# Sums of |d| by output products of two heads at a time, with |d| from ScalarE, and the rotary sum on VectorE

## The reference

```python
attn_exp = softmax(s1); attn_noise = softmax(s2)      # s1 = q k1 * SCALE, s2 = q k2 * SCALE, causal
attn = attn_exp - lam * attn_noise
denom = jnp.maximum(jnp.sum(jnp.abs(attn), axis=-1, keepdims=True), 1e-06)
attn = attn / denom
out = jnp.einsum('bhqk,bhkd->bhqd', attn, v)
```

```python
q = q * cos * scale + rotate_half(q) * sin * scale
k = k * cos / scale + rotate_half(k) * sin / scale
```

## Time and profile before

| | |
|---|---|
| median of three runs | 2244.88 us |
| profiled execution | 2240.0 us, span 2238.2 us |
| TensorE matmul busy | 1963.2 us, 88% |
| VectorE busy | 1743.6 us, 78% |
| ScalarE busy | 1389.7 us, 62% |
| GpSimd busy | 618.9 us, 28% |
| differential attention | about 36 to 794 us |
| window attention, first layer | about 816 to 1187 us |
| window attention, second layer | about 1284 to 1657 us |

### The profile page before, as it was taken

How to read it: one execution, slowest core, us unless ns; L and a number is a source line. 1 busy time by engine, 2 the same in 40 slices (tenths; PEclk the granted TensorE clock), 3 DMA queues, 4 the chain that set the end, 5 groups by cost and what they waited for, 6 DMA issues and landing times. The chain is left out here.

```text
span 2238.2 us, 43106 instructions
## 1 busy us (share of the span) xinstructions
PE 1963.2 (88%) x12640; PEld 1328.9 (59%) x12706; DVE 1743.6 (78%) x4650; ACT 1389.7 (62%) x4626; POOL 618.9 (28%) x494
## 2 busy tenths in 40 slices
PE   5999999999999947999996869999969384999998
PEld 3666656665666625777774537777745242666665
DVE  3989989899998967999993659999956737666666
ACT  2878778787787845888882338888843526333232
POOL 1101001010010135555561255555532403000000
PEclk9999999999998968999998969999989786999999
DMA  6000000000000000000001000000001000000000
GB/s 189 1 2 1 1 1 1 1 1 1 1 1 1 1 4 6 14 14 9 14 14 28 20 5 15 11 13 14 14 19 29 5 0 1 6 5 5 5 9 10
DMA packets 40718, 27.41 MB, mean 12 GB/s; under 512 B 23954, under 2 KB 33810, under 8 KB 40594
## 3 DMA queue, kind: packets, MB, share of 16 engines
q1 hardware_dynamic: 40594, 26.24, 4.5%
HBM read 10.51 MB, written 2.10 MB: 6 GB/s over the span
## 5 line engine op out<-in xcount | busy, mean ns | idle before, releaser
L391 ACT ACTIVATE a_E<-a_psS,a_nm 128x128 f32<-128x128 f32 (+1 forms) x1028 | 418.9, 429 | 29.1 <-DVE a_nm L210 29.1
L210 DVE TENSOR_REDUCE a_nm<-a_psS 128x2 f32<-128x256 f32 (+1 forms) x514 | 260.3, 548 | 58.0 <-PE a_psS L475 56.7
L471 PE MATMUL a_psS<-a_kT,a_qm 32*128 32x128 f32 (+1 forms) x2064 | 249.0, 360 | 1.9 <-ACT a_E L391 0.8
L391 ACT ACTIVATION_READ_ACCUMULATOR a_E<-a_psS,a_nm 128x1 f32 x1028 | 221.4, 215 | 0.0
L180 POOL TENSOR_TENSOR a_rs<-a_mv,minus_half 128x2 f32<-128x2 f32 x34 | 23.9, 703 | 683.6 <-DVE a_mv L260 683.6
L399 ACT ACTIVATE a_dT<-a_psT 128x384 f32<-128x384 f32 x256 | 125.8, 491 | 135.4 <-PE a_psT L484 134.1
L235 DVE SCALAR_TENSOR_TENSOR a_d<-a_E,a_cf 128x128 f32<-128x128 f32 (+1 forms) x512 | 196.4, 425 | 8.5
L1553 ACT ACTIVATE mx_sl<-mx_psG 128x512 f32<-128x512 f32 x128 | 76.1, 597 | 197.9 <-PE mx_psG L1731 197.1
L471 PEld LDWEIGHTS a_psS<-a_kT,a_qm 32*128 32x128 f32 x2064 | 140.4, 192 | 48.7 <-ACT a_E L391 28.1
L484 PE MATMUL a_psT<-ident,a_d 128*128 128x128 f32 x768 | 136.9, 289 | 32.0 <-DVE a_d L235 30.8
L792 POOL TENSOR_TENSOR b0rn<-b0ss,minus_half 128x16 f32<-128x16 f32 x36 | 107.6, 2989 | 128.3 <-DVE b0ss L832 128.3
(11 more groups left out here) (303 smaller groups left out, 4943.8 us busy)
## 6 DMA issues: line engine op xcount, KB each, us to landing
b0v<-b0v SPq DMA_DIRECT2D x34, 128.0 KB, 2.3
b1v<-b1v SPq DMA_DIRECT2D x34, 128.0 KB, 2.3
out_dram<-mx_res SPq DMA_DIRECT2D x8, 256.0 KB, 2.3
f0z<-F SPq DMA_DIRECT2D x9, 128.0 KB
f1z<-F SPq DMA_DIRECT2D x9, 128.0 KB
f0z<-F SPq DMA_DIRECT2D x9, 127.0 KB
f1z<-F SPq DMA_DIRECT2D x9, 127.0 KB
wqk<-in_wqkv_dram SPq DMA_DIRECT2D x2, 512.0 KB, 4.6
```

The lines of the kernel that those rows point to most:

```text
L210: ins = dve.tensor_reduce(nm[:, s, t, :], psS[:, s, :, (0, P)[t]:(P, 384)[t]], axis=AX.X, op=ALU.max, negate=True)
L391: ins = act.activation(E[:, s, m, c0:c1], psS[:, s, m, c0:c1], ACT.Exp, bias=nm[:, s, t, m:m + 1], accum_out=Z[:, p, h, t, m:m + 1])
L471: pe.matmul(psS[:, s, m, c0:c1], qm[rows, p, a, r, t * P:(t + 1) * P], kT[rows, p, a, 0:c1 - c0], start=(t == 0), stop=False)
```

## The change

In differential attention, |d| is no longer summed by VectorE. ScalarE evacuates psT twice, once with Copy to dT and once with Abs to a new tile aT. TensorE multiplies aT by a stationary tile `ones`, which is 1 in column 8 and 0 elsewhere, into the same psO partitions as the outputs, so that column 8 of a head's 32 is the sum of |d|. The outputs of heads h and h+1 are issued together in even steps, alternating between the two heads, each of which has its own 32 columns; the semaphore pved now counts pairs. VectorE's ab, its reduction and the sums are gone; the floor and the denominators are made once for each 128 queries, from psM, in steps 2 and 4. Two heads' buffers dT and aT are the same in number as dT's were. In window attention the rotary sum goes from GpSimd to VectorE, just ahead of `scale`, and the outputs of the two heads of a pair alternate.

```diff
-CHAIN_A = 62
+CHAIN_A = 45
...
-        ab = sb("ab", [P, 2, H, 3])
...
+        aT = sb("aT", [P, 2, 384])
+        ones = sb("ones", [P, 32])
...
-        pved = Signal(sem("pved"), H, 2)
+        pved = Signal(sem("pved"), H // 2, 1)
...
-            def absolute(pair, half, h):
-
-                s, p = h % 2, half % 2
-                dve.wait_ge(mixed.sem, mixed.at(pair, half, h % H + 1 if h >= 0 else 0))
-                own.mark(dve.tensor_reduce(ab[:, p if h >= 0 else 1 - p, h % H, :],
-                                           d[:, s, :].rearrange("p (c k) -> p c k", c=3),
-                                           axis=AX.X, op=ALU.add, apply_absolute_value=True))
...
+            def floored(pair, half, t):
 
                 q = (half - 1) % 2
+                dve.wait_ge(misc_full.sem, misc_full.at(pair, half, E_OT0 + t + 1))
+                ins = dve.scalar_tensor_tensor(out=floor[:, t, :], in0=Z[:, q, :, t, 0], scalar=1e-6,
+                                               in1=heads(t)[:, :, HD], op0=ALU.mult, op1=ALU.max)
...
                         k = inverse(pair, half, s)
-                        absolute(pair, half, s - 1)
+                        if s in (2, 4):
+                            normalise_o(s // 2 - 1)
                         k = coefficient(pair, half, s, k)
...
-                act.wait_ge(pved.sem, pved.at(pair, half, h - 1))
-                act.activation(dT[:, s, :], psT[:, s, 0:384], ACT.Copy).then_inc(evaced.sem, 1)
+                act.wait_ge(pved.sem, pved.at(pair, half, h // 2))
+                act.activation(dT[:, s, :], psT[:, s, 0:384], ACT.Copy)
+                act.activation(aT[:, s, :], psT[:, s, 0:384], ACT.Abs).then_inc(evaced.sem, 1)
...
-                pe.matmul(out[:, 0:P], vp[:, p, 0, h, :], dT[:, s, 0:P], start=True, stop=True)
-                pe.matmul(out[:, P:T], vp[:, p, 0, h, :], dT[:, s, P:T], start=True, stop=False)
-                pe.matmul(out[:, P:T], vp[:, p, 1, h, :], dT[:, s, T:384], start=False, stop=True)\
-                  .then_inc(pved.sem, 1)
+                out = lambda i: psO[32 * ((h + i) % GH):32 * ((h + i) % GH) + 32, :]
+                for i in range(2):
+                    pe.matmul(out(i), vp[:, p, 0, h + i, :], dT[:, i, 0:T], start=True, stop=False)
+                for i in range(2):
+                    pe.matmul(out(i)[:, P:T], vp[:, p, 1, h + i, :], dT[:, i, T:384], start=False, stop=False)
+                for i in range(2):
+                    pe.matmul(out(i), ones[:, :], aT[:, i, 0:T], start=False, stop=False)
+                for i in range(2):
+                    ins = pe.matmul(out(i)[:, P:T], ones[:, :], aT[:, i, T:384], start=False, stop=True)
+                ins.then_inc(pved.sem, 1)
...
-                        outputs(pair, half - 1 if s == 0 else half, (s - 1) % H)
+                        if s % 2 == 0:
+                            outputs(pair, half - 1 if s == 0 else half, (s - 2) % H)
...
-                pool.wait_ge(parts.sem, parts.at(pair, half, t + 1))
-
-                pool.wait_ge(qk_ready.sem, qk_ready.at(pair, half, t))
-                pool.tensor_tensor(rot[:, :], part[:, 0, :], part[:, 1, :], ALU.add).then_inc(summed.sem, 1)
...
+                dve.wait_ge(parts.sem, parts.at(pair, half, t + 1))
+                dve.tensor_tensor(rot[:, :], part[:, 0, :], part[:, 1, :], ALU.add).then_inc(summed.sem, 1)
                 dve.wait_ge(summed.sem, summed.at(pair, half, t + 1))
...
-                    pe.matmul(out[:, 0:P], vh(0), dT[:, s, 0:2, j, :], start=True, stop=True)
-                    pe.matmul(out[:, P:192], vh(1), dT[:, s, 2, j, :], start=True, stop=True)
-                    ins = pe.matmul(out[:, 192:T], vh(2), dT[:, s, 3, j, :], start=True, stop=True)
+                    pe.matmul(out(j)[:, 0:P], vh(j, 0), dT[:, s, 0:2, j, :], start=True, stop=True)
+                for j in range(2):
+                    pe.matmul(out(j)[:, P:192], vh(j, 1), dT[:, s, 2, j, :], start=True, stop=True)
+                for j in range(2):
+                    ins = pe.matmul(out(j)[:, 192:T], vh(j, 2), dT[:, s, 3, j, :], start=True, stop=True)
```

More of the change, by code:

```diff
@@ L174, in _ @@
         def _(pool):
-            for tile in (vp, OT, Z, ab, dT, d):
-                pool.memset(tile[:], 1.0 if tile in (Z, ab) else 0.0).then_inc(zeroed, 1)
+            for tile in (vp, OT, Z, dT, aT, d):
+                pool.memset(tile[:], 1.0 if tile is Z else 0.0).then_inc(zeroed, 1)
+            for c0, c1 in ((0, HD), (HD, HD + 1), (HD + 1, 32)):
+                pool.memset(ones[:, c0:c1], 1.0 if c0 == HD else 0.0).then_inc(zeroed, 1)
             def rstd(which, pair, half, k):
@@ L267, in normalise_x, with heads, denominators, normalise_o @@
                 ins.then_inc(xn_ready.sem, 1)
-            def sum_absolute(half):
+            def heads(t):
+                return psM[:, :].rearrange("p (h e) -> p h e", e=32)
+            def floored(pair, half, t):
                 q = (half - 1) % 2
-                own.last()
[L273 to L289, removed]
-                dve.wait_ge(misc_full.sem, misc_full.at(pair, half, E_OT0 + t + 1))
-                dve.wait_ge(den_ready.sem, den_ready.at(pair, half, 1))
-                dve.tensor_tensor(On[:, t, :].rearrange("p (h e) -> p h e", e=HD),
-                                  psM[:, :].rearrange("p (h e) -> p h e", e=32)[:, :, 0:HD],
+                dve.wait_ge(misc_full.sem, misc_full.at(pair, half, E_OT0 + t + 1))
+                ins = dve.scalar_tensor_tensor(out=floor[:, t, :], in0=Z[:, q, :, t, 0], scalar=1e-6,
+                                               in1=heads(t)[:, :, HD], op0=ALU.mult, op1=ALU.max)
+                if t == 0:
+                    own.mark(ins)
+                else:
+                    ins.then_inc(den_ready.sem, 1)
+            def denominators(pair, half, t):
+                if t == 0:
+                    own.last()
+                else:
+                    dve.wait_ge(den_ready.sem, den_ready.at(pair, half, 1))
+                own.mark(dve.reciprocal(den[:, t, :], floor[:, t, :]))
+            def normalise_o(t):
+                own.last()
+                dve.tensor_tensor(On[:, t, :].rearrange("p (h e) -> p h e", e=HD), heads(t)[:, :, 0:HD],
                                   den[:, t, :].unsqueeze(2).broadcast_to([P, H, HD]), ALU.mult)\
@@ L367, in _ @@
             own.begin(dve, LAST, 0)
-            absolute(LAST, 0, -1)
-            denominators(guard_sums(0, sum_absolute(0)))
-            normalise_o(LAST, 0, 0)
-            normalise_o(LAST, 0, 1)
+            for t in range(QT):
+                floored(LAST, 0, t)
+                denominators(LAST, 0, t)
+                normalise_o(t)
             dve.wait_ge(misc_free.sem, misc_free.at(LAST, 0, E_Y + 1))
@@ L422, in prepare @@
                          psM[:, 0:T].rearrange("p (t h e) -> p t h e", t=QT, e=HD), full)
-            act.wait_ge(zeroed, 7)
-            for signal, n in ((exped, 2), (mixed, 2), (turned, 2), (evaced, 2), (pved, 1)):
+            act.wait_ge(zeroed, 10)
+            for signal, n in ((exped, 2), (mixed, 2), (turned, 2), (evaced, 2)):
                 act.sem_inc(signal.sem, n)
@@ L487, in outputs @@
             def outputs(pair, half, h):
[L488 to L490 removed]
+                p, g = half % 2, h // GH
+                pe.wait_ge(evaced.sem, evaced.at(pair, half, h + 2))
+                if h % GH == 0:
                     pe.wait_ge(otmoved.sem, otmoved.at(pair, half, g))
[L492 to L496 removed]
+                out = lambda i: psO[32 * ((h + i) % GH):32 * ((h + i) % GH) + 32, :]
[8 more added lines that the diff above has]
+                ins.then_inc(pved.sem, 1)
             def use_misc(use, p, free):
@@ L551, in _ @@
                         turn(pair, half, s)
-            outputs(LAST, -1, H - 1)
+            outputs(LAST, -1, H - 2)
             pe.wait_ge(otmoved.sem, otmoved.at(LAST, 0, 0))
@@ L808, in _ @@
             for t in range(QT):
-                norms_and_sum(0, -1, t)
+                root_norms(0, -1, t)
             with pool.Fori(0, LAST) as pair:
@@ L815, in _ @@
                     for t in range(QT):
-                        norms_and_sum(pair, half, t)
+                        root_norms(pair, half, t)
         @block.vector
```

31 lines of the change are left out of this document (11 added, 20 removed).

## The result

The changed kernel took **2286.65 us** (median of four runs, 2282.22 to 2320.08), the kernel before 2240.62 us beside it (2232.81 to 2249.12). The ratio is **1.0198, with a 95% interval of 1.0139 to 1.0257**: slower, by 1.4 to 2.6%. A run more than 1.5% above the fastest of its kernel, as 2320.08 is here, counts as slow and stays out of the ratios. The profiled execution has a span of 2289.0 us at a mean granted clock of 0.931, against 2238.2 and 0.939 before: 50.8 us more.

A forecast was written before the change was run, and what follows sets the result against it. TensorE, full at 2.43 us a head, bounds the kernel; the change makes a closed loop bind differential attention. 2240 + 75 (differential attention) - 26 (window attention) + 5 (chains) = 2294 profiled; forecast 2296 us, range 2262 to 2340.

The forecast's parts named there:

- The closed loop, 5.78 us: Differential attention: exponentials, scores, both heads' outputs, turn and two evacuations form a circle of 5.78 us per two heads.
- What stays on the loop, 2.8 us a batch: Differential attention: psO moves, xnT and kT copies, xn transposes and K projection add 2.8 us a batch to the loop.
- The clock stays at its upper level: Differential attention: clock stays as now, since TensorE is never idle longer at a time than some 1.1 us; no cost.
- the pauses at the loop's turn: Differential attention: pauses of some 2.3 us each pair of batches, left as they are.
- Window attention, -26: Two window-attention layers: TensorE sets the pace, and alternated outputs save 0.8 us a batch, -26 us in all.
- Chains ahead of the loops, +5: Batches ahead of the window-attention loops: the rotary sum on VectorE lengthens the chain, less first L870 waits; +5 us.
- the 5 us: Whole kernel: the median of three runs lies 5 us above the profiled execution.
- (A): Differential attention: loop does not bind, engines pack by their own work, ScalarE sets 42.1 us a batch; 2184 us; chance 0.08.
- (B): Output matmuls: column groups do not overlap, two heads' outputs take 2.6 us, no window-attention gain; 2479 us; chance 0.06.
- (C): Differential attention: loop binds but nearly everything else hides in its idle time, or evacuations overlap better; 2252 us; chance 0.12.
- (D): Output matmuls: interleaving does nothing because two groups share what feeds them; 2351 us; chance 0.10.

The follow-up runs named there:

- in_turn: Changed kernel with the four output matmuls of one head issued first, then those of the other, instead of alternating; 2369.8 us.
- no_abs: Changed kernel without the second (Abs) evacuation, the matmuls with ones reading dT, so the sum of d is formed; 2211.94 us.
- no_ones: Changed kernel without the matmuls with ones, so the sum of |d| is missing from the denominator; Abs evacuation kept; 2303.76 us, ratio 1.0216.
- a_only: Kernel before with only the whole edit to differential attention, window attention as before; 2325.19 us, ratio 1.0386.
- fill: Changed kernel with eight added TensorE products of constants, which nothing reads, at heads 13 and 15; 2262.88 us, ratio 1.0119.
- rot_only: Kernel before with only window attention's rotary sum moved from GpSimd to VectorE; 2254.19 us in one run.
- inter_only: Kernel before with only window attention's output matmuls alternating between the two heads, rotary sum still on GpSimd; 2219.31 us.
- b_only: Kernel before with only the whole edit to window attention, differential attention as before; 2229.21 us, ratio 0.9979.

## Why the prediction was right

The prediction was 2296 us; it was 2286.65, inside the range, and slower.

**The closed loop, 5.78 us: right.** The links were 0.76 for 0.82, 1.72 for 1.71, 0.05 for 0.13, 1.18, 1.43 for 1.36, 0.61 for 0.58, and the pair 5.72. in_turn, no_abs and no_ones move it by the link that each changes: pairs of 6.40, 5.34 and 5.07 us. The outputs overlap in full: 6 units of 0.22 and some 0.1 ahead of the transposes, which the prediction's 0.68 for the outputs before leaves out (415.70 to 416.48 in the earlier trace rows is 0.78). The wake-up and the evacuations were put 0.14 too high, which outweighs it.

**What stays on the loop, 2.8 us a batch: right.** The steps of a batch without a pause add up to 48.53 us; less 8 x 5.72 that is 2.77. By the lengths of its steps it is also made up as said: three moves of psO at 0.26 us, copies of 0.37 and 0.48, the transposes of xn 0.29, the K projection 0.82. Against 44.31 before it is 4.2 us a batch, 67.5 in 16, where I had 75. The too large wake-up and evacuations make up the difference.

**"The clock stays at its upper level": wrong.** In the trace of the kernel before each of the seven drops of this stage stands behind a hole of 1.42 to 2.29 us of TensorE; that one of some 1.1 us would leave the clock alone does not follow from that. In the changed kernel the longest hole ahead of a drop is 0.91 to 1.14 us. Time at half clock went from 51.2 to 85.3 us, and in a_only to 146.8. It did not ruin the number because two errors met, and that is luck: the pauses at the loop's turn, which I left as they were, take less in the slack steps (the step with the pause is 2.4 us longer than its clean 2.43 in the kernel before, and 0.8 to 1.0 longer than its clean 3.38 in fill). Pauses and clock together, which is the stage less its 255 steps at their clean length, were 44.9 us and are 41.3. fill shows about what the drops cost by themselves: 29 us of differential attention. So the term that I set at nothing was two terms, one a cost and one a gain.

**Window attention, -26: -22.6.** That TensorE sets the pace, and that VectorE's freed wait is worth nothing, is shown by rot_only and inter_only. The last output matmul starts 0.45 us after the first, where I had 0.44, so each of the four outputs of a batch gives 0.27 us, as said. Of these 1.1 us a batch 0.70 arrive, not 0.8: the share that waits for copies take back was guessed, and was a third, not a quarter.

**Chains ahead of the loops, +5:** b_only has +3.1 and +2.3. The changed kernel has +7.3 and +2.3; a_only has +3.3 in the first stretch, where its window attention is unchanged. I put that down to the end of differential attention, whose last outputs, denominators and normalisation now follow one another, which no run tests; it was not priced, nor the start, 1.7 us later.

**The sum: closer than its terms.** The profiled execution was to grow by 54 us and its span grew by 50.8. Differential attention gave 63 for 75, window attention -22.6 for -26, the chains 9.6 for 5, start and end 0.7 for nothing: a term that was too large hid two that were too small in cost. Nor did the 5 us stand that were added for the median: it was 2286.65, and the profiled run 2290.85.

**The rivals.** (A), no loop, is out: TensorE waits 112 times. (B), no overlap of column groups, is out: eight matmuls take 1.43 us, and 2.6 was its figure. The rule from the Trainium skill, "TensorE: Matmul & The Clock Gate", Part 3, that a weight load overlaps a running matmul only where the row group differs, does not hold here. The step from it to 2.6 us was the prediction's own: the table of measured packings in the same Part gives a gain of 2.38 for three matmuls in different column groups, and the 1.43 us here, for 2.64 by columns, agrees with a gain. (C), all else hidden in the holes, is out: 2.77 us a batch stay. (D), nothing from alternating, is out by in_turn, whose span is 79 us longer, and by inter_only.

## What to carry to other kernels

Before packing work of two steps into one, add up the circle through all engines with each one's order as written, for an engine that is busy four fifths of the time, as ScalarE was here, can still be on it; put the bulky, unurgent work behind the step that the other engine waits for, and give it the buffers for that. A wait on an engine that does not set the pace is worth nothing, however long it is: look at which engine is full in that stage, and change that one alone. And when a change opens holes on TensorE, read the granted clock stage by stage, since holes of a microsecond can cost more than their length (in no_ones they cost the whole gain).

## What the runs showed of the hardware

The granted clock fell to 1.2 GHz though TensorE had not been idle for longer than 0.91 to 1.14 us at a time just before in the changed kernel, and 0.72 to 1.24 in no_ones. Before one fall it had been busy for 2.28 of 3.40 us. In no_ones the lower level then held for 41 us on end, through which TensorE was never idle. Adding products of constants made that kernel 85 us faster by the medians. Why the lower level mostly lasts 3.4 us in the changed kernel, 13.7 in a third of the drops of a_only and up to 44 in no_ones was not settled, nor why the drops come at other heads from batch to batch, while the same steps pass without one elsewhere.

Matmuls in different 32-column groups with all row groups in common overlap, weight loads included: eight matmuls of 256 and 128 columns took 1.43 us up to the transposes when alternated and 2.10 one head after the other, where the columns alone would give 2.64 (12 units of 0.22 us).
